# An attention and gated-FFN stage with a reordered opening, reordered rotations and maxima, and an earlier down piece

## The chip, the cores and the metric

The kernel runs on one core of one Trainium2 chip. The metric is the device time of one execution in microseconds (us); lower is better. Of several executions the median is taken.

## The reference, cut to what matters

A block of two layers over 4 x 1024 tokens of width 256. Only the second layer is touched by the change: a windowed attention with rotary embedding over 16 heads of 16, and a gated FFN whose hidden values are made 2-of-4 sparse by magnitude.

```python
x = layernorm(x + mamba_and_mlp(x))               # not touched
x = layernorm(x + mixture_of_experts(x))          # not touched except for its last layernorm
q, k, v = x @ w_q.T, x @ w_k.T, x @ w_v.T         # 16 heads of 16
q, k = rope(q), rope(k)                           # q*cos + rotated(q)*sin
attn = softmax(where(mask, q @ k.T * 0.25, -inf))
x = layernorm(x + (attn @ v) @ w_o.T)
h = silu(x @ w_gate) * (x @ w_up)                 # 1024 hidden values
h = keep_2_of_each_4_by_magnitude(h)
x = layernorm(x + h @ w_down)
```

## The kernel before, in words

The program has three phases; the third, `attention_ffn_phase`, is the one that changes. It writes out five instruction streams by hand, one for each engine, and orders them with semaphores. It works through four batches (`b` = 0 to 3) of 8 tiles of 128 tokens.

**Names.** For a tile `t` of batch `c`: `x_high` (ScalarE) and `x_low` (VectorE) split the input rows into two f16 parts; `x_transposed` (TensorE) transposes them and `xt_copied` (ScalarE) copies that out; `qkv` (TensorE, 12 matmuls at L1864) makes q, k and v; `qkv_copied` (ScalarE) evicts them; `rotate` (VectorE, four instructions, L1583 to L1590) applies the rotary embedding into the tile `ro`; `high_part` and `part_copies` (ScalarE) and `low_parts` (VectorE, L1596, L1597) write the split parts into `qks`. `first_rows` transposes them for the first head group. `for_maximum` (TensorE) makes one block of scores for the running row maximum and `maximum` (VectorE, L1607 and L1612) reduces it; a group of heads has 2 x `NX` = 40 of them, and the PSUM tile that they use has two halves, so that `for_maximum(m)` waits for `maximum(m - 2)`. `max_parts` closes each twenty. `weight_high` (ScalarE) and `weight_low` (VectorE, L1569) split the weights, which lie raw in the scratch tile `room`.

**The opening.** Before batch 0 there is nothing to overlap with. VectorE makes two layernorms (`stats`, `normal`), whose inverse deviations come from GpSimd (`inverse_deviation`). GpSimd then fills constant columns of `v` and `qks` (L1353 to L1356). Eight tiles pass through the chain above, then `first_rows`, the 40 maxima of the first head group, and `heads(0)`.

**One batch.** `heads(b)` is the attention. Then come the output projection and 16 chunks of hidden values (`w` = 0 to 15): TensorE `hidden(b, w)` (12 matmuls at L2059 into a ring of two PSUM tiles), ScalarE `silu`, VectorE `hidden` (the gated product, L1660), ScalarE `magnitude`. A chunk's matmuls wait until the gated product of two chunks before is done. Each four chunks are sparsified on VectorE by `compare` (L1670 to L1672), `count` (L1677 to L1685) and `keep_largest` (L1694), together `sparsify`, and then feed a down piece, `down(b, k)` with 16 calls (32 matmul records at L2072), k = 0 to 3, which waits for `keep_largest` of the same k. Pieces 0 and 1 make the first half of the tokens, which `residual(b, 0)` adds; 2 and 3 the second. In batches 0 to 2 the qkv and rotations of the next batch are interleaved with chunks 0 to 7, and the 40 maxima of its first head group with the later chunks and down pieces. This is what `ahead` stands for; the last batch has none of it. On TensorE the callbacks `among_hidden`, `at_end_of_first` and `at_end_of_second` place single `for_maximum` calls between matmuls.

```python
if w == (12 if ahead else DOWN_AT):
    down(b, 0, nothing)
    down(b, 1, at_end_of_first)
hidden(b, w, among_hidden)
...
down(b, 2, nothing)
if ahead:
    wait(pe, hm_ok, 16 * c)
    q_max_transposed(c, 0, 0)
down(b, 3, at_end_of_second)
```

Of the kernel before, what the change touches and what calls it, by code (L numbers as in the profile page):

```python
# [1157 lines left out]
def attention_ffn_phase(nc, io, keep):  # L1158
    with ExitStack() as ctx:  # L1159
# [173 lines left out]
        def _(pool):  # L1333
# [14 lines left out]
            pool.memset(power[:], -0.5)  # L1348
# [17 lines left out]
        def _(act):  # L1366
# [28 lines left out]
            def high_part(c, t):  # L1395
# [77 lines left out]
            act.sem_inc(ev_ok, LEAD)  # L1473
            weight_high(0, "w_qk")
# [4 lines left out]
            for t in range(ST):  # L1479
# [4 lines left out]
                if t in (1, 2):  # L1484
                    weight_high(t + 1, ("w_fg", "w_fu")[t - 1])
# [54 lines left out]
        def _(dve):  # L1540
# [36 lines left out]
            def rotate(c, t):  # L1577
# [180 lines left out]
            for t in range(ST):  # L1758
# [3 lines left out]
                low_parts(0, t)  # L1762
            weight_low(2, "w_fg")
            weight_low(3, "w_fu")
            maxima(0, 0, 0, 2 * NX)
            for b in range(NB):
# [21 lines left out]
                for w in range(NF + 1 if ahead else 16):  # L1788
                    if ahead and w + 1 < ST:
# [444 lines left out]
```

## Time and profile before

| what | value |
|---|---|
| median of 3 runs | 1815.56 us (1813.19 to 1816.39) |
| the profiled execution's own time | 1813.41 us |
| its span, first to last instruction | 1811.6 us |
| mean granted TensorE clock | 0.929 of 2.4 GHz |
| third phase | 687 to 1811.6 us |
| its opening, to the first scores of `heads(0)` | 687 to 787 us |

All times in the text are microseconds from the start of the span of the profiled execution. L1864 is line 1864 of the kernel. "Granted clock" is the share of TensorE's full clock that the chip granted: 1.00 is 2.4 GHz and 0.50 is 1.2 GHz. A row of the timeline merges instructions of one kind that ran back to back; a bracket behind it gives the engine's idle time before it and what released it.

### The profile page before, as it was taken

To read this page: it belongs to the slowest core of one execution; us is meant where nothing else is said; L and a number is where in the kernel's file an instruction comes from. 1 tells how busy PE (TensorE), PEld (TensorE's weight loads), DVE (VectorE), ACT (ScalarE), POOL (GpSimd) and SP (SyncE) were. 2 spreads that over 40 slices of the span, in tenths; PEclk is the share of its full clock that TensorE was granted. 3 is DMA by queue.
4 is the path that set the end of the run, shared out by engine and by line. 5 is a ranking of instruction groups with operands and counts; after the bars stand their busy time and mean duration, and the time that the engine had idled before them with its cause. 6 is when DMAs were issued, how large, how long until landed. Compare 5 with 4: busy or idle time off the path is not lost.

```text
span 1811.6 us, 27446 instructions
## 1 busy us (share of the span) xinstructions
PE 1542.5 (85%) x10490; PEld 961.8 (53%) x10491; DVE 1153.6 (64%) x2399; ACT 822.2 (45%) x1352; POOL 234.8 (13%) x237
## 2 busy tenths in 40 slices
PE   3999999977989973589888989888989888989796
PEld 2899988864568772233344534254534344433355
DVE  5566666637421145678568778668778678778475
ACT  5444444512212213347855157744157753177530
POOL 5334444412400001000000000100000100000000
PEclk8999999978999986669999989989999999989999
DMA  2000000105215502000000000000000000000000
GB/s 107 12 25 24 23 23 24 34 12 174 51 37 148 153 1 96 1 1 2 1 1 1 0 1 1 25 1 1 1 1 1 24 1 1 1 1 2 24 1 24
DMA packets 27153, 48.04 MB, mean 27 GB/s; under 512 B 7312, under 2 KB 16016, under 8 KB 26256
## 3 DMA queue, kind: packets, MB, share of 16 engines
q1 hardware_dynamic: 26464, 44.74, 7.7%
q0 software_dynamic: 576, 1.77, 0.4%
q8 instruction: 74, 1.21, 0.3%
q14 instruction: 39, 0.32, 0.1%
HBM read 37.59 MB, written 9.06 MB: 26 GB/s over the span
## 4 chain that ended last, share of the span: by engine, by line
issue 60%; POOL 2%; DVE 0%; POOLq 0%; DVEq 0%
POOL rs_sb L1340 1%; POOL ve_sb L1337 0%; POOL qks_sb L1355 0%; POOL v_sb L1354 0%; POOL qks_sb L1345 0%; DVE bn_sb L1545 0%; DVE x_sb_sb L1560 0%; POOLq L1159 0%; POOLq L65 0%; POOL qks_sb L1356 0%; DVE mv_sb L1551 0%; DVEq L1159 0%; POOL v_sb L1353 0%; DVE ident_h_sb L1742 0%; DVEq L65 0%
## 5 line engine op out<-in xcount | busy, mean ns | idle before, releaser
L1612 DVE TENSOR_REDUCE mx_sb<-s_ps 128x1 f32<-128x512 f32 (+1 forms) x512 | 312.8, 652 | 111.9 <-PE s_ps L1906 65.0
L1418 ACT ACTIVATE room_sb<-s_ps 128x1024 f32<-128x1024 f32 (+1 forms) x320 | 283.5, 949 | 23.7 <-PE s_ps L1930 22.5
L1903 PE MATMUL s_ps<-room_sb 48*128 48x512 f16 (+3 forms) x640 | 177.1, 343 | 39.9 <-DVE mx_sb L1607 20.0
L1903 PEld LDWEIGHTS s_ps<-room_sb 48*128 48x128 f16 x640 | 52.9, 96 | 210.3 <-DVE mx_sb L1612 126.4
L1930 PE MATMUL s_ps<-room_sb 51*128 51x128 f16 (+4 forms) x1152 | 145.3, 283 | 22.3 <-ACT room_sb L1418 14.9
L1950 PE MATMUL cm_ps<-room_sb,v_sb 128*32 128x512 f32 (+3 forms) x1536 | 162.3, 511 | 0.8 <-ACT room_sb L1424 0.8
L1337 POOL TENSOR_TENSOR ve_sb<-mv_sb,eps_sb 128x4 f32<-128x4 f32 x24 | 5.0, 210 | 1081.5 <-DVE mv_sb L1551 1081.5
L2072 PE MATMUL cm_ps<-w_fd_sb,room_sb 128*128 128x256 f32 x512 | 131.4, 406 | 14.7 <-DVE room_sb L1694 14.7
L394 DVE SCALAR_TENSOR_TENSOR x_sb_sb<-xp_sb,conv_w_sb,x_sb_sb 128x512 f32<-128x512 f32 x96 | 109.2, 1139 | 22.6 <-ACT x_sb_sb L319 20.5
L2072 PEld LDWEIGHTS cm_ps<-w_fd_sb,room_sb 128*128 128x128 f32 x512 | 97.3, 198 | 38.4 <-issue 14.0
L2059 PE MATMUL s_ps<-xbT_sb,w_fg_sb 128*128 128x512 f16 x384 | 100.3, 391 | 10.2 <-DVE ctok_sb L1660 8.7
L2059 PE MATMUL s_ps<-xbT_sb,w_fu_sb 128*128 128x512 f16 x384 | 103.3, 400 | 0.0
L965 PE MATMUL em_ps<-xT_sb,ws_gu_sb 128*128 128x512 f32 x192 | 90.4, 616 | 7.8 <-DMA rows<-zeros 7.8
L1930 PEld LDWEIGHTS s_ps<-room_sb 50*128 50x128 f16 (+1 forms) x1152 | 54.7, 97 | 79.0 <-ACT room_sb L1418 49.9
L1906 PE MATMUL s_ps<-room_sb 51*128 51x128 f16 x512 | 83.0, 233 | 10.5 <-ACT room_sb L1408 10.0
L400 DVE SCALAR_TENSOR_TENSOR m1T_sb<-mm_ps,m1T_sb 128x512 fp32r<-128x512 f32 x64 | 44.1, 688 | 66.1 <-ACT m1T_sb L311 65.8
L1464 ACT ACTIVATE sgl_sb<-s_ps 128x512 f32<-128x512 f32 x64 | 37.9, 593 | 85.5 <-PE s_ps L2059 85.3
L1607 DVE TENSOR_REDUCE mx_sb<-s_ps 128x2 f32<-128x512 f32 (+1 forms) x128 | 66.0, 554 | 13.3 <-PE s_ps L1906 13.0
L488 PE MATMUL ro_ps<-w_dn_sb,m1T_sb 128*128 128x256 f32 x256 | 71.6, 280 | 0.0
L489 PE MATMUL ro_ps<-w_dn_sb,m1T_sb 128*128 128x256 f32 x256 | 71.6, 280 | 0.0
L490 PE MATMUL ro_ps<-w_dn_sb,m1T_sb 128*128 128x256 f32 x256 | 71.5, 279 | 0.0
L311 ACT ACTIVATE m1T_sb<-mm_ps 128x512 fp32r<-128x512 f32 x64 | 37.9, 593 | 66.3 <-PE mm_ps L490 66.3
(255 smaller groups left out, 3194.6 us busy)
## 6 DMA issues: line engine op xcount, KB each, us to landing
we_gu_sb<-we_gu SPq DMA_DIRECT2D x32, 352.0 KB
we_dn_sb<-we_dn SPq DMA_DIRECT2D x32, 176.0 KB
x_in_sb<-x SPq DMA_DIRECT2D x9, 512.0 KB, 3.5
rows<-x_sb_sb SPq DMA_DIRECT2D x8, 512.0 KB, 3.0
x_sb_sb<-rows SPq DMA_DIRECT2D x2, 2048.0 KB, 12.0
out<-x_sb_sb SPq DMA_DIRECT2D x8, 512.0 KB, 2.6
xp_sb<-w_in SPq DMA_DIRECT2D x1, 1024.0 KB, 5.7
x_sb_sb<-w_up SPq DMA_DIRECT2D x1, 1024.0 KB, 7.3
```

The costliest lines, as they stand in the source:

```text
L394: dve.scalar_tensor_tensor(xc[:, c, :], xp[:, c, k:k + GTOK], conv_w[:, c, k:k + 1], xc[:, c, :], ALU.mult, ALU.add)\
L488: pe.matmul(out, of[0][at], by[0][cols], start=start, stop=False)
L489: pe.matmul(out, of[1][at], by[0][cols], start=False, stop=False)
L965: last = pe.matmul(mm[c % 4][:, :], ws_gu[:, k, col:col + P], xT[:, k, g * GTOK:(g + 1) * GTOK], start=(k == 0), stop=(k == KD - 1))
L1418: act.activation(weights[(g * NU + u) % SLOTS_P][:, 2 * pair:2 * pair + 2, 0:width(u) * P], W[s % 2][:, :, 0:width(u) * P], ACT.Exp, scale ...
L1612: dve.tensor_reduce(mx[:, pair, k % 2, slot:slot + 1], X[:, k % 2, 0:count * P], AX.X, ALU.max, negate=True).then_inc(mx_ok, 1)
L1903: last = pe.matmul(X[:, k % 2, at * P:(at + plain) * P], query[head:head + NORM, i * P:(i + 1) * P], key[head:head + NORM, j * P:(j + plai ...
L1906: last = pe.matmul(X[:, k % 2, (at + plain) * P:(at + count) * P], query[head:head + USED, i * P:(i + 1) * P], key[head:head + USED, i * P ...
L1930: last = pe.matmul(W[s % 2][:, head, (at + low - i) * P:(at + high - i) * P], key[first:first + rows, j * P:(j + 1) * P], query[first:firs ...
L1950: last = pe.matmul(O[32 * h:32 * h + 32, (i - half * GT) * P:(i - half * GT + count) * P], v[:, j, g * HG + h, :], weights[(g * NU + u) % ...
L2059: last = pe.matmul(bank[:, e, :], wt[:, j, k, ch * P:(ch + 1) * P], xh[:, g, k, i, :], start=(k == n == 0), stop=(k == KD - 1 and n == 2))
L2072: last = pe.matmul(CM[:, t // 2, (t % 2) * D:(t % 2 + 1) * D], hs[:, k % 3 * 4 + i, t * P:(t + 1) * P], w_fd[:, k % 2 * 4 + i, :], start=( ...
```

## The change

1. Opening, fills: the four fills of `v` and `qks` go from GpSimd's memsets to ScalarE activations, ahead of its first weight copy.
2. Opening, order on VectorE: the first half's layernorm, the second half's statistics, then `x_low` of tiles 0 and 1, the two weight parts, and only then the second half's `normal`.
3. Opening, tiles: rotated tiles alternate between `ro` and the tile `sgl`, so that `low_parts` of tile t - 1 stands behind `rotate` of tile t on VectorE.
4. Opening, FFN weights: the copies `weight_high` 2 and 3 go from among the tiles to behind the first four `qk_copied` on ScalarE; `weight_low` 2 and 3 go from ahead of the first twenty maxima to behind them on VectorE.
5. Batches 0 to 2, chunks 5 and 6: VectorE makes the gated product before the rotation. `keep_largest` of the first four chunks goes from behind product 6 to behind product 7.
6. Batches 0 to 2: TensorE makes down piece 0 ahead of chunk 10 (before: ahead of chunk 12, next to piece 1). No maxima stand among chunks 10 and 11. Maxima 0 to 7 stand in the second half of down piece 1, 8 to 23 among chunks 12 to 15, 24 to 39 in all of down piece 3 (before: 0 to 7 among chunks 10 and 11, 8 to 11 in the last quarter of piece 1, 12 to 27 among chunks 12 to 15, 28 to 39 in three quarters of piece 3). VectorE's order follows.

```diff
@@ gpsimd
-            pool.memset(v[:, :, :, HD:HD + 1], 1.0)
-            pool.memset(v[:, :, :, HD + 1:], 0.0).then_inc(setup, 1)
-            pool.memset(qks[:, :, :, USED:], 0.0)
-            pool.memset(qks[:, :, :, NORM:FILTER], UNIT).then_inc(setup, 1)
@@ scalar
+            def filled(out, value):
+                own = power[:, 0:1].unsqueeze(2).unsqueeze(3).to_broadcast([P, ST, out.shape[2], out.shape[3]])
+                return act.activation(out, own, ACT.Copy, scale=value / POWER)
+            act.wait_ge(setup, 1)
+            filled(v[:, :, :, HD:HD + 1], 1.0)
+            filled(v[:, :, :, HD + 1:], 0.0).then_inc(setup, 1)
+            filled(qks[:, :, :, USED:], 0.0)
+            filled(qks[:, :, :, NORM:FILTER], UNIT).then_inc(setup, 1)
             weight_high(0, "w_qk")
...
-                if t in (1, 2):
-                    weight_high(t + 1, ("w_fg", "w_fu")[t - 1])
...
                 for s in (1, 0):
                     qk_copied(0, 0, pair, s)
+            weight_high(2, "w_fg")
+            weight_high(3, "w_fu")
@@ vector
+        def turned_tile(c, t):
+            return sgl[:, 0, :].rearrange("p (h d) -> p h d", h=2 * HEADS) if c == 0 and t % 2 else ro[:, :, :]
...
-                wait(dve, ca_ok, k)
-                wait(dve, low_ok, k)
+                wait(dve, ca_ok, k if c > 0 else k - 1)
+                wait(dve, low_ok, k if c > 0 else k - 1)
...
-            for s in range(2):
-                layernorm("x", 0, s)
+            layernorm("x", 0, 0)
+            stats("x", 0, 1)
+            x_low(0, 0)
+            x_low(0, 1)
             weight_low(0, "w_qk")
             weight_low(1, "w_v")
-            x_low(0, 0)
-            x_low(0, 1)
+            normal("x", 0, 1)
...
                 rotate(0, t)
-                low_parts(0, t)
+                if t > 0:
+                    low_parts(0, t - 1)
+            low_parts(0, ST - 1)
+            maxima(0, 0, 0, NX)
             weight_low(2, "w_fg")
             weight_low(3, "w_fu")
-            maxima(0, 0, 0, 2 * NX)
+            maxima(0, 0, NX, 2 * NX)
...
-                    if ahead and w + 1 < ST:
+                    if ahead and w < TURN_LATE:
                         rotate(c, w + 1)
...
                     hidden(b, w)
+                    if ahead and TURN_LATE <= w < ST - 1:
+                        rotate(c, w + 1)
...
-                    if w >= 4 and w % 4 == 2:
+                    if w >= 4 and w % 4 == (3 if ahead else 2):
                         keep_largest(b, w // 4 - 1)
...
-                    for w in range(10, 12):
-                        m = 4 * (w - 10)
-                        maxima(c, 0, m, m + 2)
-                        hidden(b, w - 1)
-                        if w == 10:
-                            keep_largest(b, 1)
-                        maxima(c, 0, m + 2, m + 4)
+                    hidden(b, 9)
+                    keep_largest(b, 1)
+                    hidden(b, 10)
                     hidden(b, 11)
                     sparsify(b, 2)
-                    maxima(c, 0, 8, 12)
+                    maxima(c, 0, 0, 8)
                     residual(b, 0)
                     for w in range(12, 16):
-                        m = 4 * (w - 9)
+                        m = 4 * (w - 10)
...
-                    maxima(c, 0, 28, 2 * NX)
+                    maxima(c, 0, 24, 2 * NX)
@@ tensor
-                    if ahead and w in (10, 11):
-                        for_maximum(c, 0, 4 * (w - 10) + i)
                     if ahead and w >= 12:
-                        for_maximum(c, 0, 4 * (w - 9) + i)
+                        for_maximum(c, 0, 4 * (w - 10) + i)
...
-                    if ahead and t == GT - 1:
-                        for_maximum(c, 0, 8 + i)
+                    if ahead and t >= GT - 2:
+                        for_maximum(c, 0, 4 * (t - GT + 2) + i)
...
-                    if ahead and t > 0:
-                        for_maximum(c, 0, 28 + 4 * (t - 1) + i)
+                    if ahead:
+                        for_maximum(c, 0, 24 + 4 * t + i)
...
+                    if ahead and w == FIRST_DOWN:
+                        down(b, 0, nothing)
+                    if not ahead and w == DOWN_AT:
+                        down(b, 0, nothing)
                     if w == (12 if ahead else DOWN_AT):
-                        down(b, 0, nothing)
                         down(b, 1, at_end_of_first)
```

The constants are `TURN_LATE = 5`, `FIRST_DOWN = 10`, `POWER = -0.5`, and `GT` is 4. `high_part`, `part_copies` and `low_parts` read `turned_tile(c, t)` where they read `ro`.

## Rows read from the trace of the kernel before

**Rows 1.** The page: busy time, share of the span and instructions of each engine.

```profile
PE 1542.5 (85%) x10490; PEld 961.8 (53%) x10491; DVE 1153.6 (64%) x2399; ACT 822.2 (45%) x1352; POOL 234.8 (13%) x237
```

**Rows 2.** Stretches: length; busy PE, PEld, DVE, ACT, POOL; clock, DMA, GB/s.

```profile
704.50:755.30 50.80, 27.61 (x128) 13.94 (x128) 25.68 (x65) 26.13 (x56) 0.00 (x0) 0.70 0.00 0
...
755.30:787.00 31.70, 25.23 (x114) 9.44 (x115) 27.27 (x44) 4.90 (x5) 0.00 (x0) 0.50 0.00 1
...
970.30:994.50 24.20, 18.55 (x101) 7.46 (x100) 20.65 (x38) 10.10 (x17) 0.00 (x0) 0.86 0.00 1
...
1027.20:1053.00 25.80, 22.45 (x94) 14.08 (x92) 17.62 (x28) 2.11 (x3) 0.00 (x0) 0.93 0.00 1
```

**Rows 3.** Timeline of the opening, VectorE: start, length, line, tile, count.

```profile
696.38 6.20 DVE L1560 TENSOR_SCALAR x_sb_sb<-x_sb_sb,mv_sb,rs_sb 128x256 f32<-128x256 f32 x4 [1.49 <-POOL rs_sb L1340]
...
702.50 1.21 DVE L1569 SCALAR_TENSOR_TENSOR w_qk_sb<-room_sb,w_qk_sb 128x1024 f16<-128x1024 f32 x1
...
704.23 0.75 DVE L1575 TENSOR_TENSOR xs_sb<-x_sb_sb,xs_sb 128x256 f16<-128x256 f32 x2
```

**Rows 4.** Timeline of the opening, GpSimd: the longest of its fills.

```profile
698.07 2.87 POOL L1355 MEMSET qks_sb<- 128x3328 f16 x1
```

**Rows 5.** Line 1560 over the whole span: ns min/median/max, first and last start.

```profile
L1560 DVE TENSOR_SCALAR x_sb_sb<-x_sb_sb,mv_sb,rs_sb x96: 395/408/5173, 691.6 to 1808.2; 128x256 f32<-128x256 f32 x96
```

**Rows 6.** Timeline of the opening, ScalarE: two weight copies.

```profile
691.72 1.06 ACT L1369 ACTIVATE w_qk_sb<-room_sb 128x1024 f16<-128x1024 f32 x1 [43.89 <-DMA room_sb<-w_v]
...
712.11 1.92 ACT L1369 ACTIVATE w_fg_sb<-room_sb 128x2048 f16<-128x2048 f32 x1
```

**Rows 7.** Timeline of the opening's tiles, TensorE (in brackets: idle before, releaser).

```profile
706.53 2.77 PE L1864 MATMUL s_ps<-w_qk_sb,xt_sb 128*128 128x512 f16 x6
...
736.05 0.61 PE L1851 MATMUL s_ps<-ident_h_sb,xs_sb 128*128 128x128 f16 x4 [2.61 <-DVE xs_sb L1575]
...
736.45 2.77 PE L1864 MATMUL s_ps<-w_qk_sb,xt_sb 128*128 128x512 f16 x6
...
739.01 1.49 PE L1864 MATMUL s_ps<-w_v_sb,xt_sb 128*128 128x256 f16 x6
...
743.34 1.46 PE L1864 MATMUL s_ps<-w_qk_sb,xt_sb 128*128 128x512 f16 x6
```

**Rows 8.** Timeline of the opening's tiles, VectorE.

```profile
741.96 0.42 DVE L1596 TENSOR_TENSOR qks_sb<-ro_sb,qks_sb 128x256 f16<-128x256 f32 x1 [3.96 <-ACT qks_sb L1399]
...
742.63 0.42 DVE L1575 TENSOR_TENSOR xs_sb<-x_sb_sb,xs_sb 128x256 f16<-128x256 f32 x1
...
744.63 0.42 DVE L1590 TENSOR_TENSOR ro_sb<-ro_sb,sn_sb 128x256 f32<-128x256 f32 x1
```

**Rows 9.** Timeline after the last tile, VectorE: weight part, then maxima.

```profile
754.95 2.29 DVE L1569 SCALAR_TENSOR_TENSOR w_fg_sb<-room_sb,w_fg_sb 128x2048 f16<-128x2048 f32 x1
...
763.43 10.65 DVE L1612 TENSOR_REDUCE mx_sb<-s_ps 128x1 f32<-128x384 f32 x16
```

**Rows 10.** Timeline of batch 0's hidden chunks, TensorE, chunk 8.

```profile
973.36 2.72 PE L2059 MATMUL s_ps<-xbT_sb,w_fg_sb 128*128 128x512 f16 x6 [2.90 <-DVE ctok_sb L1660]
```

**Rows 11.** Timeline of batch 0, TensorE: down pieces and around them.

```profile
981.00 1.06 PE L1870 MATMUL s_ps<-ident_h_sb,qks_sb 128*128 128x128 f16 x16
...
994.53 12.79 PE L2072 MATMUL cm_ps<-w_fd_sb,room_sb 128*128 128x256 f32 x58
...
1010.43 0.82 PE L2059 MATMUL s_ps<-xbT_sb,w_fg_sb 128*128 128x512 f16 x3
...
1027.22 7.17 PE L2072 MATMUL cm_ps<-w_fd_sb,room_sb 128*128 128x256 f32 x32
...
1038.19 4.01 PE L2072 MATMUL cm_ps<-w_fd_sb,room_sb 128*128 128x256 f32 x10 [3.35 <-DVE room_sb L1694]
...
1042.45 0.70 PE L2072 MATMUL cm_ps<-w_fd_sb,room_sb 128*128 128x256 f32 x2
...
1043.41 0.70 PE L2072 MATMUL cm_ps<-w_fd_sb,room_sb 128*128 128x256 f32 x2
```

**Rows 12.** Timeline of batch 0, VectorE: product 9 and the third sparsification.

```profile
985.96 0.68 DVE L1660 SCALAR_TENSOR_TENSOR room_sb<-s_ps,sgl_sb 128x512 f32<-128x512 f32 x1
...
996.49 1.76 DVE L1670 TENSOR_TENSOR room_sb<-room_sb 128x1536 bf16<-128x1536 f32 x1 [0.69 <-ACT room_sb L1470]
...
1002.96 2.50 DVE L1694 SCALAR_TENSOR_TENSOR room_sb<-nb_sb,room_sb 128x512 f32<-128x512 bf16 x4
```

More of the change, by code:

```diff
@@ L1114 @@
 HALF_AT = 3
+TURN_LATE = 5
+FIRST_DOWN = 10
 DOWN_AT = 13
@@ L1127 @@
 W_SCALE = 64.0
+POWER = -0.5
 PRODUCTS = ((0, 0), (1, 0), (0, 1))
@@ L1346, in zero_columns @@
                 last.then_inc(zeroed, 1)
-            pool.memset(power[:], -0.5)
+            pool.memset(power[:], POWER)
             pool.memset(eps[:], 1e-5).then_inc(setup, 1)
@@ L1398, in high_part @@
                     wait(act, tm_mm, 2 * NHG * c)
-                act.activation(part(t, None, 0), ro[:, :, :], ACT.Copy).then_inc(a_ok, 1)
+                act.activation(part(t, None, 0), turned_tile(c, t), ACT.Copy).then_inc(a_ok, 1)
             def part_copies(c, t):
-                act.activation(part(t, 0, 2), by_head(ro[:, :, :])[:, :, 0, :, :], ACT.Copy)
-                act.activation(part(t, 1, 1), by_head(ro[:, :, :])[:, :, 1, :, :], ACT.Copy).then_inc(ca_ok, 1)
+                act.activation(part(t, 0, 2), by_head(turned_tile(c, t))[:, :, 0, :, :], ACT.Copy)
+                act.activation(part(t, 1, 1), by_head(turned_tile(c, t))[:, :, 1, :, :], ACT.Copy).then_inc(ca_ok, 1)
             def qk_copied(b, g, pair, s):
@@ L1580, in rotate @@
                 wait(dve, qkv_ok, k + 1)
-                wait(dve, ca_ok, k)
-                wait(dve, low_ok, k)
-                dve.tensor_tensor(ro[:, :, :], x, cos[:, t, :].unsqueeze(1).to_broadcast([P, 2 * HEADS, HD]),
+                wait(dve, ca_ok, k if c > 0 else k - 1)
+                wait(dve, low_ok, k if c > 0 else k - 1)
+                own = turned_tile(c, t)
+                dve.tensor_tensor(own, x, cos[:, t, :].unsqueeze(1).to_broadcast([P, 2 * HEADS, HD]),
                                   ALU.mult).then_inc(turned, 1)
@@ L1588, in rotate @@
                 wait(dve, turned, 2 * k + 2)
-                dve.tensor_tensor(ro[:, :, 0:HALF_D], ro[:, :, 0:HALF_D], sn[:, :, HALF_D:], ALU.add)
-                dve.tensor_tensor(ro[:, :, HALF_D:], ro[:, :, HALF_D:], sn[:, :, 0:HALF_D], ALU.add).then_inc(rv_ok, 1)
+                dve.tensor_tensor(own[:, :, 0:HALF_D], own[:, :, 0:HALF_D], sn[:, :, HALF_D:], ALU.add)
+                dve.tensor_tensor(own[:, :, HALF_D:], own[:, :, HALF_D:], sn[:, :, 0:HALF_D], ALU.add).then_inc(rv_ok, 1)
             def low_parts(c, t):
@@ L1594, in low_parts @@
                 wait(dve, rv_ok, c * ST + t + 1)
-                own = by_head(ro[:, :, :])
+                own = by_head(turned_tile(c, t))
                 dve.tensor_tensor(part(t, 0, 1), own[:, :, 0, :, :], part(t, 0, 0), ALU.subtract)
@@ L2100, in among_hidden @@
                         x_transposed(c, w + 2)
-                    if ahead and w in (10, 11):
+                    if ahead and w >= 12:
                         for_maximum(c, 0, 4 * (w - 10) + i)
-                    if ahead and w >= 12:
-                        for_maximum(c, 0, 4 * (w - 9) + i)
                 def at_end_of_first(t, i):
-                    if ahead and t == GT - 1:
-                        for_maximum(c, 0, 8 + i)
+                    if ahead and t >= GT - 2:
+                        for_maximum(c, 0, 4 * (t - GT + 2) + i)
                 def at_end_of_second(t, i):
-                    if ahead and t > 0:
-                        for_maximum(c, 0, 28 + 4 * (t - 1) + i)
+                    if ahead:
+                        for_maximum(c, 0, 24 + 4 * t + i)
                 heads(b)
```

## The prediction

> **What bounds the kernel.** I read the page first, for the engines' shares: TensorE is busy 85% of the span, VectorE 64%, ScalarE 45%, GpSimd 13% [rows 1]. That is an average, so I went on to stretches, and then to the timeline of each engine in the two places that the change touches.
>
> The opening is a chain and no engine is full. From 704.5 to 755.3 us TensorE is busy 27.6 of 50.8 us, VectorE 25.7, ScalarE 26.1 [rows 2]. The reader is to see what each waits for. A tile goes round one loop: its transposes wait for `x_low` (2.61 us idle), and VectorE can't give the next `x_low` because it stands in `low_parts`, 3.96 us idle for the `high_part` that ScalarE makes only after the next tile's qkv [rows 7, 8]. From 755.3 to 787 VectorE is busy 27.3 of 31.7 us with maxima and is the bound [rows 2, 9].
>
> In the batches TensorE is nearly full, and the losses are a few waits for VectorE: 2.90 us ahead of chunk 8 [rows 10], 24.2 us for 18.6 busy from there to down piece 0 [rows 2], and 3.35 us ahead of piece 3 [rows 11]. After such waits the granted clock is below 1.00 (0.86 and 0.93 in those stretches [rows 2]).
>
> **The opening's fills and order.** The second `normal` took 6.20 us for four instructions [rows 3], one of them 5.17 us where the median is 0.41 [rows 5]. That stretch is the one in which GpSimd fills, the longest fill being 2.87 us [rows 4]. VectorE was held by the fills, and this goes. (The Trainium skill, "SBUF — State Buffer", on the shared port pair, says that GpSimd and some VectorE instructions take it as an exclusive lock. The 5.17 us agree. The sum uses the row, so it would be the same without the page.) The fills now cost ScalarE: 1.06 us for 1024 elements and 1.92 for 2048 [rows 6] make some 0.2 us plus 0.84 per thousand; 128 + 1920 + 3328 + 512 elements in four instructions are 5.7 us, 5.4 with the overlap of neighbours. Bounds: nothing beyond its idle time until 691.72 [rows 6], or twice that if strided writes are slow, which would delay the first qkv by some 5 us. I take 5.4, since the rows are of the same kind. ScalarE then goes from 687.4 to 692.8, makes two weight copies to 694.4 and two `x_high` to 695.1. VectorE's statistics end at 694.9 (696.38 less 1.49 idle [rows 3]), `x_low` of two tiles at 695.6, and the two weight parts (702.50 to 704.23 [rows 3]) at 697.4. The first qkv starts at 697.5 instead of 706.53 [rows 7]: **9.0 us gained**.
>
> **The tiles.** With `low_parts` one tile late, VectorE's work per tile is `x_low` and the four rotation instructions, 742.63 to 744.97 with the last of 744.63 [rows 8], and `low_parts`, 741.96 to 742.63: 3.0 us, 3.15 with handovers. ScalarE's seven copies are 2.9. TensorE's tile is 4.45 us at the lower clock (0.4 for the transposes, then 736.45 to 740.5) and 2.2 at the higher, where the q and k part is 1.46 instead of 2.77 [rows 7]. So the period is 3.15 at 2.4 GHz and 4.45 at 1.2 GHz; before it was 6.2 to 7.1. Laid out from 697.5: the rotations of tiles 0 and 1 start at 702.25 and 704.7, six periods follow, and rotation 7, `low_parts` 6 and 7 take 3.5. At the higher clock the last `low_parts` ends at 727.1, at the lower at 734.9. The granted clock was 0.70 over this stretch [rows 2], so I take the middle, 3.8 a period: 731. That is 33.5 us instead of 48.5 (706.53 to 755.0): **15.0 us gained**, bounds 11 and 19. (The Trainium skill, "TensorE: Matmul & The Clock Gate", Part 1, says that the array is at half rate until activity releases it. Taken by itself it would have the denser loop at the higher clock, and the gain 19; no row before shows this loop dense.)
>
> **The FFN weights.** The two `weight_low` of 2.29 us [rows 9] stood where VectorE would have waited for the transposes and copies of q and k in any case. Now they stand between the twentieth and the twenty-first maximum. There maxima follow each other without a gap, 16 in 10.65 us [rows 9], and TensorE can be only two ahead. What is queued behind is the second twenty, then `heads(0)`. **4.4 us lost.** The ScalarE copies, 3.8 us, are hidden: their next work, `q_max_copied`, waits some 13 us for the first twenty maxima. Opening in all: -9.0 - 15.0 + 4.4 = **-19.6**, bounds -24 and -15.
>
> **Gated products ahead of rotations.** Product 5 ahead of rotation 6 puts that rotation, and through ScalarE's queue the next `silu`, some 0.7 us later; product 6 ahead of rotation 7 takes 2.0 us (one rotation, [rows 8]) from ahead of it. Net, product 6 comes 1.3 us earlier. Chunk 8 starts at 972.0 instead of 973.36 [rows 10]. Then `keep_largest` stands ahead of product 8, and `count` of the second four ends at 986.5, so product 9 is at 986.5 instead of 985.96 [rows 12]. The 1.4 us gained on TensorE are real there, and end in the next wait.
>
> **Down piece 0 ahead of chunk 10.** Batch 0 laid out: chunk 9 and its transposes end at 980.7 (before 981.9 [rows 11]). `keep_largest` of the first four is long done, so piece 0 fills 980.7 to 987.75 (7.05 us: 7.17 in [rows 11] with its modelled end). Chunks 10 and 11 take 2.6 each, to 992.95. Piece 1 starts there. Its first half and two slots with maxima are done at 998.1, and maximum 2 waits for VectorE's reduction of maximum 0. That stands behind product 11 (994.3) and all of the third sparsification: `compare` from 995.0 instead of 996.49, 8.97 us as before (996.49 to 1005.46 [rows 12]), to 1003.95. TensorE idles **6.2 us** in the middle of piece 1. Five slots of 0.95 us (1042.45 to 1043.41 [rows 11]) with what is left of this one bring piece 1's end to 1009.3. The row of chunk 12 before is 1010.43. The other waits of this size before, 2.90 and 3.35 us, were each followed by slow matmuls: 2.72 us for six after the first, against 1.46, and 4.01 us for ten records after the second, where a piece runs 32 in 7.17 [rows 10, 11]. I take 1.8 us for that, and chunk 12 at 1011.1. So the 5.6 us of waits that go from ahead of piece 0 come back inside piece 1. Bounds for chunk 12 against before: -1.1 (no slow matmuls) and +0.7 us; I take +0.3.
>
> **The moved maxima.** Chunks 12 to 15 get larger maxima: +0.2. Piece 3 gets four more: a slot with a maximum is 0.95 us, one without is 7.05 / 16 = 0.44, so +2.0. They were in chunks 10 and 11 beside waits; piece 3 has nothing to hide them. The wait ahead of piece 3 stays, since the sparsification follows product 15 as before. Each of batches 0, 1 and 2 (the same waits stand in all three) costs 0.3 + 0.2 + 2.0 = 2.5, **+7.5** in all; bounds +3 (by -1.1) and +9 (by +0.7), widened to 0 and +12 for waits that my layout may miss. Batch 3 has no edit.
>
> **Sum.** -19.6 + 7.5 = **-12.1 us** on an execution of 1813.41 (1.8 of it outside the span). The median of the runs is 2.15 above that one, so I forecast 1815.56 - 12.1 = 1803.5.
>
> **Rivals.**
> The forecast has chance 0.50: opening about -20, batches +2 to +3 each; 1800 to 1808.
>
> *The batches are neutral and the tiles run at 2.4 GHz* (0.27). For it: at 743.34 the clock did rise though TensorE waited in every period [rows 7], and the 9.7 us of idle and slow time between chunk 8 and piece 0 are more than the 6.2 that I put in. Against it: the third sparsification is fixed by product 11. It gives -24 + 1 = -23, 1792.
>
> *The tiles stay at 1.2 GHz and the fills are slow* (0.14). For it: clock 0.50 through 755 to 787 with TensorE 80% busy [rows 2]. It gives -9 - 11 + 4.4 + 3 = -12.6 for the opening; with +9 for the batches -3.6, 1812.
>
> *Slower than before* (0.08): the stall inside piece 1. If the clock stays at the lower level after the 6.2 us, through the 16 quarters of chunks 12 to 15, each quarter of 1.07 us grows by 0.7, 11 us a batch, 33 in all. It decides from 6.5 us a batch. Against it: after 3.35 us idle the clock was back within ten records [rows 11]. It gives -19.6 + 7.5 + 33 = +21, 1836.
>
> *No change* (0.01): it needs the tile loop to have another bound than `low_parts`; the 3.96 us wait speaks against that.
>
> **Chances.** A measurement here tells 0.2%, 3.6 us, from no change. Faster: 0.50 + 0.27 + most of 0.14 = 0.88. Same 0.04, slower 0.08. The range takes in the first three cases but their tails: 1790 to 1812.
>
> **What would show it.** First qkv near 697.5; no `normal` instruction over 0.5 us there; last `low_parts` 27 to 34 us after it; a gap of 4.4 us in the maxima; `heads(0)` 20 us earlier. In batch 0, relative to chunk 7: a wait of some 6 us inside piece 1, on a maximum; piece 3 some 15 us long with 16 maxima; each batch 2 to 3 us longer. The prediction is wrong if that wait is absent or the clock stays down behind it, or if the fills hold ScalarE beyond 695 us.

## The result, and the profile after

The changed kernel took 1852.7 us in the median (four runs, 1841.2 to 1854.5) against 1814.9 for the kernel before: ratio 1.0163, 95% interval 1.0126 to 1.0201. That is 30 us slower by the ratio and 38 by the two medians, where 12 us faster was forecast. Beside the experiments below the kernel before had medians of 1818.6 to 1821.5 us, so they are compared by their ratios to it. The page of the kernel after, its span and its first part:

```profile
span 1852.6 us, 27445 instructions
...
PE 1594.9 (86%) x10490; PEld 981.2 (53%) x10491; DVE 1151.2 (62%) x2399; ACT 827.1 (45%) x1356; POOL 229.6 (12%) x233
```

TensorE is busy 52 us more [rows 1] for the same 10490 instructions; VectorE has 2 us less. The mean granted clock is 0.898 instead of 0.929.

Where the time went is read from GpSimd, whose small `ve` instruction marks every layernorm. The timeline of GpSimd, kernel after: the start of the third phase, the first layernorm inside `heads(0)`, and the first ones inside `heads(1)` to `heads(3)`:

```profile
693.41 0.10 POOL L1355 MEMSET power_sb<- 128x4 f32 x1 [51.41 <-POOLq L615]
...
885.43 0.20 POOL L1344 TENSOR_TENSOR ve_sb<-mv_sb,eps_sb 128x4 f32<-128x4 f32 x1 [182.45 <-DVE mv_sb L1563]
...
1158.15 0.20 POOL L1344 TENSOR_TENSOR ve_sb<-mv_sb,eps_sb 128x4 f32<-128x4 f32 x1 [241.90 <-DVE mv_sb L1563]
...
1444.80 0.20 POOL L1344 TENSOR_TENSOR ve_sb<-mv_sb,eps_sb 128x4 f32<-128x4 f32 x1 [243.12 <-DVE mv_sb L1563]
...
1731.52 0.20 POOL L1344 TENSOR_TENSOR ve_sb<-mv_sb,eps_sb 128x4 f32<-128x4 f32 x1 [243.18 <-DVE mv_sb L1563]
```

The same marks before stand at 687.19, 902.92, 1157.96, 1426.13 and 1690.21. So the first two phases, which nothing touches, took 6.2 us more in this execution; the opening and `heads(0)` up to the mark took 192.0 us instead of 215.7, **23.7 us less**; and the three stretches between the marks took 17.7, 18.5 and 22.6 us more, **58.8 us in all**. 6.2 - 23.7 + 58.8 is 41.3, the difference of the two spans (41.0) to within 0.3 us.

**The opening after.** TensorE, kernel after, answering to [rows 7]:

```profile
703.64 2.72 PE L1879 MATMUL s_ps<-w_qk_sb,xt_sb 128*128 128x512 f16 x6
...
713.80 0.40 PE L1866 MATMUL s_ps<-ident_h_sb,xs_sb 128*128 128x128 f16 x4 [0.66 <-DVE xs_sb L1587]
...
717.23 0.40 PE L1866 MATMUL s_ps<-ident_h_sb,xs_sb 128*128 128x128 f16 x4 [1.09 <-DVE xs_sb L1587]
...
733.76 1.87 PE L1885 MATMUL s_ps<-ident_h_sb,qks_sb 128*128 128x128 f16 x16 [5.79 <-DVE qks_sb L1610]
```

VectorE, kernel after, answering to [rows 3, 9]:

```profile
703.41 1.37 DVE L1572 TENSOR_SCALAR x_sb_sb<-x_sb_sb,mv_sb,rs_sb 128x256 f32<-128x256 f32 x4
...
752.71 2.28 DVE L1581 SCALAR_TENSOR_TENSOR w_fg_sb<-room_sb,w_fg_sb 128x2048 f16<-128x2048 f32 x1
754.91 2.28 DVE L1581 SCALAR_TENSOR_TENSOR w_fu_sb<-room_sb,w_fu_sb 128x2048 f16<-128x2048 f32 x1
```

ScalarE's fills, kernel after:

```profile
693.58 2.03 ACT L1479 ACTIVATE v_sb<-power_sb 128x128 f32<-128x128 f32 x2 [40.04 <-POOL eps_sb L1356]
695.51 3.50 ACT L1479 ACTIVATE qks_sb<-power_sb 128x3328 f16<-128x3328 f32 x2
```

The first qkv starts 10.2 us behind the phase's start instead of 19.3. The second `normal` takes 1.37 us. The fills are 5.3 us of ScalarE (693.58 to 698.89). Tiles go by in 3.0 and 3.4 us, all but the first at the higher clock. `first_rows` starts 40.4 us behind the phase's start instead of 68.2. The two FFN weight parts stand in the maxima, 752.71 to 757.11.

**A batch after.** Stretches of the kernel after; columns as in [rows 2]. They are the opening's tiles, piece 1 to the end of its wait, the rest of piece 1, chunks 12 to 15, and piece 3:

```profile
703.60:733.80 30.20, 19.63 (x121) 10.78 (x122) 25.65 (x66) 21.55 (x53) 0.00 (x0) 0.90 0.08 32
974.99:986.55 11.56, 5.73 (x27) 4.05 (x26) 9.94 (x18) 1.23 (x2) 0.00 (x0) 0.87 0.00 0
986.55:995.09 8.54, 8.54 (x26) 3.68 (x27) 3.33 (x6) 0.00 (x0) 0.00 (x0) 0.50 0.00 0
995.09:1014.50 19.41, 19.41 (x77) 5.52 (x76) 13.60 (x23) 3.68 (x7) 0.00 (x0) 0.86 0.00 1
...
1025.61:1052.60 26.99, 26.99 (x61) 9.98 (x61) 10.15 (x16) 0.00 (x0) 0.00 (x0) 0.50 0.00 0
```

TensorE around them, kernel after, answering to [rows 10, 11]:

```profile
954.44 1.46 PE L2074 MATMUL s_ps<-xbT_sb,w_fg_sb 128*128 128x512 f16 x6 [1.48 <-DVE ctok_sb L1673]
...
974.99 4.05 PE L2087 MATMUL cm_ps<-w_fd_sb,room_sb 128*128 128x256 f32 x18
...
986.55 0.28 PE L1918 MATMUL s_ps<-room_sb 48*128 48x128 f16 x1 [5.83 <-DVE mx_sb L1620]
...
987.08 1.22 PE L2087 MATMUL cm_ps<-w_fd_sb,room_sb 128*128 128x256 f32 x2
...
1025.61 1.22 PE L2087 MATMUL cm_ps<-w_fd_sb,room_sb 128*128 128x256 f32 x2 [3.48 <-DVE room_sb L1707]
...
1027.19 1.22 PE L2087 MATMUL cm_ps<-w_fd_sb,room_sb 128*128 128x256 f32 x2
```

VectorE there, kernel after, answering to [rows 12]:

```profile
977.20 1.76 DVE L1683 TENSOR_TENSOR room_sb<-room_sb 128x1536 bf16<-128x1536 f32 x1 [0.69 <-ACT room_sb L1473]
...
983.66 2.49 DVE L1707 SCALAR_TENSOR_TENSOR room_sb<-nb_sb,room_sb 128x512 f32<-128x512 bf16 x4
986.08 0.75 DVE L1620 TENSOR_REDUCE mx_sb<-s_ps 128x2 f32<-128x256 f32 x2
```

The reader is to see two numbers. Behind the wait of 5.83 us inside piece 1 each call of the piece is 1.22 us where it was 0.70 ahead of it, and the matmuls stay slow up to the fourth quarter of chunk 12. And **piece 3 takes 26.99 us at a granted clock of 0.50 from its first call to its last**, against 14.91 us before (1038.19 to 1053.10). With chunk 7 as the common start (967.71 before, 950.21 after), batch 0 lost 2.2 us up to chunk 12, 2.6 in chunks 12 to 15 (19.41 instead of 16.79), 0.1 in piece 2 and its wait, and 12.1 in piece 3: 17.0 of 17.7. In all three batches together piece 3 lost 36 of the 58.8 us. (Piece 3 took 15.0 us in each batch before and 27.0 in each after, counted to the transposes behind it.)

The row of piece 3 shows TensorE busy 26.99 of 26.99 us. Busy time says nothing there of the pace. (The Trainium skill, "Trainium Kernel Development and Optimization", Performance Expectations, calls matmul busy time a bad metric for how close a kernel is to roofline. This piece agrees: fully busy both times, 14.9 and 27.0 us.)

### The profile page after: what moved, and what is told of

It reads as the page before. It is cut to its first block, busy times and chain, and to the rows that moved or that the text cites. A ratio compares the mean times of both kernels' runs of the same rounds, so it can differ in the third digit from the quotient of the medians.

```text
span 1852.6 us, 27445 instructions
## 1 busy us (share of the span) xinstructions
PE 1594.9 (86%) x10490; PEld 981.2 (53%) x10491; DVE 1151.2 (62%) x2399; ACT 827.1 (45%) x1356; POOL 229.6 (12%) x233
## 4 chain that ended last, share of the span: by engine, by line
issue 60%; POOL 2%; DVE 0%; POOLq 0%; DVEq 0%
POOL rs_sb L1347 1%; POOL ve_sb L1344 0%; DVE bn_sb L1557 0%; POOL qks_sb L1352 0%; DVE x_sb_sb L1572 0%; POOLq L1162 0%; POOLq L65 0%; DVE mv_sb L1563 0%; DVEq L1162 0%; DVE ident_h_sb L1755 0%; DVEq L65 0%; DVEq L1561 0%; DVEq L1754 0%; DVEq L1753 0%; DVEq L1752 0%
## 5 line engine op out<-in xcount | busy, mean ns | idle before, releaser
L1625 DVE TENSOR_REDUCE mx_sb<-s_ps 128x1 f32<-128x512 f32 (+1 forms) x512 | 313.7, 652 | 145.2 <-PE s_ps L1921 79.6
L1918 PE MATMUL s_ps<-room_sb 48*128 48x512 f16 (+3 forms) x640 | 189.5, 363 | 54.3 <-DVE mx_sb L1620 35.0
L2087 PE MATMUL cm_ps<-w_fd_sb,room_sb 128*128 128x256 f32 x512 | 166.1, 468 | 15.0 <-DVE room_sb L1707 15.0
L2087 PEld LDWEIGHTS cm_ps<-w_fd_sb,room_sb 128*128 128x128 f32 x512 | 104.9, 222 | 49.1 <-issue 25.4
L394 DVE SCALAR_TENSOR_TENSOR x_sb_sb<-xp_sb,conv_w_sb,x_sb_sb 128x512 f32<-128x512 f32 x96 | 109.2, 1140 | 22.6 <-ACT x_sb_sb L319 20.5
L1921 PE MATMUL s_ps<-room_sb 51*128 51x128 f16 x512 | 88.5, 245 | 6.3 <-ACT room_sb L1411 5.9
L1620 DVE TENSOR_REDUCE mx_sb<-s_ps 128x2 f32<-128x512 f32 (+1 forms) x128 | 66.2, 553 | 24.0 <-PE s_ps L1921 23.7
L1411 ACT ACTIVATE room_sb<-s_ps 128x1024 f16<-128x1024 f16 x24 | 23.2, 1023 | 104.1 <-PE s_ps L1885 104.1
## 6 DMA issues: line engine op xcount, KB each, us to landing
x_sb_sb<-rows SPq DMA_DIRECT2D x2, 2048.0 KB, 11.4
```

The lines of the kernel that those rows point to most:

```text
L394: dve.scalar_tensor_tensor(xc[:, c, :], xp[:, c, k:k + GTOK], conv_w[:, c, k:k + 1], xc[:, c, :], ALU.mult, ALU.add)\
L1625: dve.tensor_reduce(mx[:, pair, k % 2, slot:slot + 1], X[:, k % 2, 0:count * P], AX.X, ALU.max, negate=True).then_inc(mx_ok, 1)
L1918: last = pe.matmul(X[:, k % 2, at * P:(at + plain) * P], query[head:head + NORM, i * P:(i + 1) * P], key[head:head + NORM, j * P:(j + plai ...
L1921: last = pe.matmul(X[:, k % 2, (at + plain) * P:(at + count) * P], query[head:head + USED, i * P:(i + 1) * P], key[head:head + USED, i * P ...
L2087: last = pe.matmul(CM[:, t // 2, (t % 2) * D:(t % 2 + 1) * D], hs[:, k % 3 * 4 + i, t * P:(t + 1) * P], w_fd[:, k % 2 * 4 + i, :], start=( ...
```

## The experiments

**The two halves apart.** First the opening's edits alone: parts 1 to 4 as in the change, the batches as in the kernel before.

> The opening's edits alone (parts 1 to 4), batches as before. In the profile after, the first layernorm inside heads(0) stands 23.7 us earlier relative to the start of the third phase (192.0 instead of 215.7 us), while the batches lose some 60. Theory A (the opening's gain is real and independent of the batches): faster than before by 22 to 25 us. Rival B (part of that gain is given back once heads(0) starts): 5 to 15 us faster, or none.

Measured: 1794.5 us, ratio 0.9855 (0.9817 to 0.9893), 26 us faster. GpSimd's marks:

```profile
687.71 0.10 POOL L1355 MEMSET power_sb<- 128x4 f32 x1 [49.81 <-POOLq L615]
...
878.86 0.20 POOL L1344 TENSOR_TENSOR ve_sb<-mv_sb,eps_sb 128x4 f32<-128x4 f32 x1 [181.58 <-DVE mv_sb L1563]
```

191.2 us from the phase's start to the mark, 24.6 less than before. Theory A holds; the opening's gain is kept.

Then parts 5 and 6 alone behind the old opening.

> Parts 5 and 6 alone, opening as before. Theory A (losses come from the batches, 17.7, 18.5 and 22.6 us in the profile after): 55 to 65 us slower than before. Rival B (the two halves of the change interact, and the batches lose less behind the old opening): under 45 us slower.

Measured: 1870.2 us, ratio 1.0284 (1.0245 to 1.0324), 52 us slower: a little under the 55 that theory A allowed, well above B's 45. The first mark stands 216.4 us behind the phase's start (215.7 before), and the three stretches between the marks are 20.1, 15.2 and 19.3 us longer than before. With -26 the halves give +25, and together they measured +30 with intervals of some 7 us to either side: they add up.

This run also shows something that the changed kernel doesn't. Piece 3 of its batches 1 and 2 begins with one call at the higher clock, right behind the wait, and is slow from the second call on; 15 of the 16 calls take 1.22 us. TensorE, batch 1:

```profile
1330.60 0.70 PE L2072 MATMUL cm_ps<-w_fd_sb,room_sb 128*128 128x256 f32 x2 [3.48 <-DVE room_sb L1696]
...
1331.50 1.22 PE L2072 MATMUL cm_ps<-w_fd_sb,room_sb 128*128 128x256 f32 x2
```

**Is it the clock or the number of maxima?** The kernel before with one edit, on TensorE: the same 12 maxima, a quarter of the piece earlier.

```diff
 def at_end_of_second(t, i):
-    if ahead and t > 0:
-        for_maximum(c, 0, 28 + 4 * (t - 1) + i)
+    if ahead and t < GT - 1:
+        for_maximum(c, 0, 28 + 4 * t + i)
```

> The kernel before with one edit on TensorE: the 12 maxima in down piece 3 stand in its first three quarters instead of its last three. The number of instructions, of maxima and of waits is the same. Theory A (with a maximum behind each call from the first on, TensorE stays at 1.2 GHz after the wait ahead of piece 3, where four calls without maxima had let the clock rise): piece 3 takes some 23 us instead of 14.9, and the run is 20 to 30 us slower than before. Rival B (piece 3 is long because it has 16 maxima and their handovers, not 12): no change beyond 3 us.

Measured: 1838.2 us, ratio 1.0117 (1.0071 to 1.0163), 21 us slower. TensorE, batch 0 of this run, piece 3, and its stretch with columns as in [rows 2]:

```profile
1037.59 1.22 PE L2072 MATMUL cm_ps<-w_fd_sb,room_sb 128*128 128x256 f32 x2 [3.35 <-DVE room_sb L1694]
...
1039.28 1.22 PE L2072 MATMUL cm_ps<-w_fd_sb,room_sb 128*128 128x256 f32 x2
...
1057.84 3.54 PE L2072 MATMUL cm_ps<-w_fd_sb,room_sb 128*128 128x256 f32 x8
...
1037.60:1061.40 23.80, 23.80 (x52) 9.90 (x52) 8.89 (x15) 0.00 (x0) 0.00 (x0) 0.51 0.00 0
```

Twelve maxima and sixteen calls as before, and the piece takes 23.8 us (1037.59 to 1061.38) instead of 14.9, at 1.22 us a call and 1.69 a slot until the calls without maxima come. Rival B is out, and VectorE is not the bound: its reductions take 0.69 us and wait some 1.0 us for TensorE before each. Only the place of the four bare calls differs: first before, last here.

Next, 14 matmuls whose results nobody reads, in the changed kernel's wait ahead of piece 3.

```diff
+def spin(times):
+    for n in range(times):
+        pe.matmul(S[0][:, 0, :], w_fg[:, 0, 0, 0:P], xh[:, 0, 0, 0, :], start=True, stop=True)
 ...
     q_max_transposed(c, 0, 0)
+    spin(14)
 down(b, 3, at_end_of_second)
```

> The changed kernel with 14 extra matmuls of 512 columns on TensorE, whose results are not used, in the 3.5 us wait ahead of down piece 3 of batches 0 to 2. Theory A (the clock): the wait is filled, TensorE enters piece 3 at 2.4 GHz, piece 3 takes 15 to 16 us instead of 27, and the run is 30 to 36 us faster than the changed kernel, 1817 to 1823. Rival B (maxima and handovers): piece 3 stays at 25 us or more, and the run is within 3 us of the changed kernel or slower.

Measured: 1818.7 us, ratio 0.9994 (0.9958 to 1.0030), 31 us under the changed kernel by the ratios. TensorE, batch 0 of this run:

```profile
1016.68 3.19 PE L2115 MATMUL s_ps<-xbT_sb,w_fg_sb 128*128 128x512 f16 x14
1020.32 0.70 PE L2087 MATMUL cm_ps<-w_fd_sb,room_sb 128*128 128x256 f32 x2 [0.46 <-DVE room_sb L1707]
...
1034.36 0.70 PE L2087 MATMUL cm_ps<-w_fd_sb,room_sb 128*128 128x256 f32 x2
```

The idle time ahead of the piece shrinks to 0.46 us, every call of the piece is 0.70 again, and the piece with its 16 maxima takes 15.2 us, in all three batches. Some 30 us of the 59 were the clock in piece 3 alone.

The same filling in the kernel before with the maxima in front:

> The run with the kernel before's 12 maxima in the first three quarters of down piece 3, plus 14 unused matmuls of 512 columns in the wait ahead of that piece. Theory A (the clock alone made that kernel slow): piece 3 takes 14 us or less and the run is back at the level of the kernel before or up to 6 us faster. Rival B (maxima ahead in the piece cost by their place): it stays 10 us or more slower than before.

Measured: 1816.4 us, ratio 0.9972 (0.9934 to 1.0010): back at the level of before. TensorE, batch 0 of this run, and the stretch of the piece:

```profile
1038.03 0.70 PE L2072 MATMUL cm_ps<-w_fd_sb,room_sb 128*128 128x256 f32 x2 [0.33 <-DVE room_sb L1694]
...
1049.43 1.99 PE L2072 MATMUL cm_ps<-w_fd_sb,room_sb 128*128 128x256 f32 x8
...
1038.00:1051.30 13.30, 13.27 (x48) 6.19 (x48) 8.91 (x15) 0.00 (x0) 0.00 (x0) 1.00 0.00 0
```

11.4 us for the twelve slots and 13.4 for the piece, at a granted clock of 1.00 where it was 0.51. The same order of calls is 10.4 us shorter by the filling alone.

**The wait inside piece 1.** The changed kernel with both waits filled.

```diff
 def at_end_of_first(t, i):
+    if ahead and t == GT - 2 and i == 2:
+        wait(pe, hm_ok, 16 * b + 11)
+        spin(26)
```

(The `wait` makes sure that the product has been read from the PSUM tile that the unused matmuls overwrite. The 14 of the run before stay.)

> The changed kernel with unused matmuls in both waits: 14 ahead of down piece 3, as in the run before this, and 26 in the wait for maximum 0 inside down piece 1. The wait inside piece 1 lasted 5.8 us and was followed by 14 us at 1.2 GHz, to the middle of chunk 12. Theory A (the rest of the loss is clock too): piece 1 goes on at 2.4 GHz, 5 to 7 us less for each batch, and the run is 15 to 20 us faster than with the first filling alone, 1799 to 1804. Rival B (only piece 3 was a clock matter; piece 1 is bound by the reductions on VectorE): within 4 us of 1819.

Measured: 1799.0 us, ratio 0.9884 (0.9860 to 0.9908), 20 us below the first filling. TensorE, batch 0 of this run:

```profile
975.12 5.78 PE L2115 MATMUL s_ps<-xbT_sb,w_fg_sb 128*128 128x512 f16 x26
...
981.45 0.70 PE L2087 MATMUL cm_ps<-w_fd_sb,room_sb 128*128 128x256 f32 x2
...
986.01 0.82 PE L2074 MATMUL s_ps<-xbT_sb,w_fg_sb 128*128 128x512 f16 x3
```

Calls of 0.70 us right behind the wait, and chunk 12 at 986.01, where it is 995.09 in the changed kernel with a third phase that began 5.2 us later: 3.9 us earlier within the phase. Chunks 12 to 15 take 17.0 us instead of 19.4, so this is 6.3 us a batch, as A said. What TensorE has to wait for comes no sooner: from the first unused matmul to `for_maximum(2)` it is 6.0 us, since that time is VectorE's.

With both waits filled the kernel is at 0.9884, and the opening alone without any filling was at 0.9855 (0.9817 to 0.9893). So even at the higher clock parts 5 and 6 show no gain.

**Piece 3's first quarter without maxima, no fillings.** The four maxima go to piece 1. The cut shows TensorE; VectorE's order follows.

```diff
 def at_end_of_first(t, i):
-    if ahead and t >= GT - 2:
-        for_maximum(c, 0, 4 * (t - GT + 2) + i)
+    if ahead and t > 0:
+        for_maximum(c, 0, 4 * (t - 1) + i)
 def at_end_of_second(t, i):
-    if ahead:
-        for_maximum(c, 0, 24 + 4 * t + i)
+    if ahead and t > 0:
+        for_maximum(c, 0, 28 + 4 * (t - 1) + i)
```

> The changed kernel, down piece 0 still ahead of chunk 10, but with the four maxima taken out of the first quarter of piece 3: piece 1 has maxima 0 to 11 in its last three quarters, chunks 12 to 15 have 12 to 27, piece 3 has 28 to 39 in its last three quarters as in the kernel before. No extra matmuls. Theory A: piece 3 takes 15 us again instead of 27 and the run is 25 to 36 us faster than the changed kernel, 1817 to 1828, what is left being the wait and the slow clock in piece 1. Rival B (the early piece 0 is what costs, through the wait in piece 1): little changes, 1840 or more.

Measured: 1836.6 us, ratio 1.0086 (1.0066 to 1.0107), 14 us under the changed kernel. That is between the two expectations. TensorE, batch 0 of this run: the first slow call in piece 1, chunk 12, and piece 3:

```profile
987.57 1.22 PE L2087 MATMUL cm_ps<-w_fd_sb,room_sb 128*128 128x256 f32 x2
...
1002.33 1.46 PE L2074 MATMUL s_ps<-xbT_sb,w_fg_sb 128*128 128x512 f16 x3
...
1032.53 4.63 PE L2087 MATMUL cm_ps<-w_fd_sb,room_sb 128*128 128x256 f32 x10 [3.35 <-DVE room_sb L1707]
...
1047.54 0.70 PE L2087 MATMUL cm_ps<-w_fd_sb,room_sb 128*128 128x256 f32 x2
```

Piece 3 is 16 us instead of 27; A said 15. But piece 1 now waits 7.56 us instead of 5.83, has nine slow calls in place of five, and lasts to 1002.33, which is 6.8 us later behind the phase's start. Of the 11 us that piece 3 won, piece 1 lost 7: the maxima moved from one slow stretch into another.

**Part 5 alone.** Gated products ahead of rotations, in the kernel before.

> Part 5 alone in the kernel before: gated products 5 and 6 ahead of rotations, and keep_largest of the first four chunks behind product 7. By the layout in the prediction chunk 8 starts 1.4 us earlier and the gain ends in the next wait. Theory A: within 3 us of before. Rival B (a shorter wait ahead of chunk 8, 1.5 us where it was 2.9, keeps the clock at 2.4 GHz and this carries on): 3 to 8 us faster.

Measured: 1824.5 us, ratio 1.0020 (1.0000 to 1.0040). TensorE, batch 0 of this run: chunk 8, and piece 3's start:

```profile
979.91 1.46 PE L2062 MATMUL s_ps<-xbT_sb,w_fg_sb 128*128 128x512 f16 x6 [1.48 <-DVE ctok_sb L1661]
...
1045.61 4.11 PE L2075 MATMUL cm_ps<-w_fd_sb,room_sb 128*128 128x256 f32 x10 [3.35 <-DVE room_sb L1695]
```

The wait ahead of chunk 8 is 1.48 us instead of 2.90 and its six matmuls take 1.46 us instead of 2.72 [rows 10]. Nothing of this is left in the total, which is the same or slightly longer: piece 3 comes 65.7 us behind chunk 8 here, 64.8 before, so the next waits took back 0.9 us of it (those inside chunks 10 and 11 are 3.7 us together, 2.7 before), and the rest doesn't show.

**The opening's parts.** Part 1 alone:

> Part 1 alone in the kernel before: the four fills as ScalarE activations, VectorE's order as before. Theory A (GpSimd's fills held the second normal, 6.20 us for 1.38 of work, and ScalarE's fills cost less than that): the second normal takes 1.4 us, the weight parts and the first qkv come 4 to 5 us earlier, the run is 3 to 5 us faster than before, at the edge of what can be told. In the profile the first layernorm inside heads(0) stands 211 us behind the start of the third phase instead of 215.7. Rival B (normal is slow for another reason, or the longer ScalarE queue delays the splits): 0 to 2 us.

Measured: 1816.2 us, ratio 0.9976 (0.9950 to 1.0003). VectorE, the second `normal` of this run:

```profile
703.07 1.38 DVE L1565 TENSOR_SCALAR x_sb_sb<-x_sb_sb,mv_sb,rs_sb 128x256 f32<-128x256 f32 x4 [1.49 <-POOL rs_sb L1340]
```

The mark stands 210.1 us behind the phase's start (693.88 to 904.02), 5.6 less than before, a little over A's 5; the total is at the edge of what can be told. In the kernel before the one long `normal` instruction ran from 696.38 to 701.55, and GpSimd's second to fourth fill, back to back, from 696.38 to 701.40. So VectorE was held across three fills, not for the longest of 2.87 us alone [rows 4].

Part 3 alone:

> Part 3 alone in the kernel before: a second tile for the rotated rows in the opening, low_parts one tile late. The copies of the FFN weights stay among the tiles and ahead of the maxima. Theory A (the wait of VectorE in low_parts bounded the loop): the tile period falls from 6 to 7 us to 3.2 to 3.5 at the higher clock, first qkv to last low_parts from 48.5 to about 31 to 34 us; 14 to 18 us faster. Rival B (the weight copies among the tiles, 3.8 us of ScalarE, or the clock, become the bound): 10 us or less.

Measured: 1797.0 us, ratio 0.9884 (0.9823 to 0.9945), 21 us faster, where A said 14 to 18; the mark is 16.9 us nearer, and the rest is within the interval. TensorE: the longest period of a tile, 4.5 us, where the copies of the FFN weights stand among the tiles, and `first_rows`:

```profile
718.07 0.40 PE L1858 MATMUL s_ps<-ident_h_sb,xs_sb 128*128 128x128 f16 x4 [1.68 <-DVE xs_sb L1579]
...
722.55 0.40 PE L1858 MATMUL s_ps<-ident_h_sb,xs_sb 128*128 128x128 f16 x4 [2.13 <-DVE xs_sb L1579]
...
739.08 1.87 PE L1877 MATMUL s_ps<-ident_h_sb,qks_sb 128*128 128x128 f16 x16 [5.80 <-DVE qks_sb L1602]
```

First qkv (706.61) to `first_rows` is 32.5 us, inside A.

**Two versions for speed.** The opening alone with the waits ahead of chunk 8 and piece 3 filled:

> The opening's edits alone, batches as before, and unused matmuls in two waits of each batch: 12 ahead of chunk 8 (wait of 2.9 us), 14 ahead of down piece 3 (3.35 us). Theory A (slow matmuls behind a wait cost 1.3 us at chunk 8 and 2.2 us at piece 3): 8 to 11 us faster than the opening alone, about 1784 to 1787. Rival B (the slow stretches hide under other waits, as the gain of an earlier chunk 8 would): 3 us or less.

Measured: 1791.7 us, ratio 0.9833 (0.9787 to 0.9880). That is 4 us less than the opening alone, between A and B and within the spread of the runs. In the profile piece 3 takes 13.3 us in every batch, where it is 14.7, 15.0 and 16.3 in the opening alone, so that gain doesn't hide under later waits. But stretches of unchanged code around it ran at another clock: from the end of piece 3 of batch 1 to the next mark 109.6 us at a granted clock of 0.89, in the opening alone 106.1 at 0.94.

The last takes out part 4 as well, and keeps only the filling ahead of piece 3. Cut to part 4, against the changed kernel:

```diff
+                if t in (1, 2):
+                    weight_high(t + 1, ("w_fg", "w_fu")[t - 1])
...
-            maxima(0, 0, 0, NX)
             weight_low(2, "w_fg")
             weight_low(3, "w_fu")
-            maxima(0, 0, NX, 2 * NX)
+            maxima(0, 0, 0, 2 * NX)
```

> A version for speed: the opening's parts 1 to 3, with the FFN weight copies left among the tiles and weight_low left ahead of the maxima as in the kernel before (part 4 out), batches as before, and 14 unused matmuls in the wait ahead of down piece 3. Theory A (part 4 cost 4.4 us in the maxima and gives some 2.5 us back in the tiles; a warm start of piece 3 is worth some 2 us a batch): the first layernorm inside heads(0) stands 189 to 190 us behind the start of the third phase, against 191.2 for the opening alone, and the run is at 1786 to 1792. Rival B (the copies among the tiles cost as much as they save, and the slow start of piece 3 is hidden): no difference from the opening alone, 1794.

Measured: 1782.4 us (1779.3 to 1786.1), ratio 0.9802 (0.9779 to 0.9826), 36 us faster than before, and the fastest of all. GpSimd's marks:

```profile
687.26 0.10 POOL L1355 MEMSET power_sb<- 128x4 f32 x1 [48.41 <-POOLq L615]
...
876.41 0.20 POOL L1344 TENSOR_TENSOR ve_sb<-mv_sb,eps_sb 128x4 f32<-128x4 f32 x1 [179.58 <-DVE mv_sb L1563]
```

189.2 us between them, 2.0 less than for the opening alone, as expected. The total is below A's 1786 to 1792; the 2 us of the opening don't account for it. Between the marks this profile is 11.3 us shorter than that of the opening alone: 6.0 of it in the three pieces 3, the rest in stretches with the same code, of which the three ahead of the pieces ran at a granted clock of 1.00, 0.97 and 0.97 against 0.97, 0.94 and 0.96. Why that clock differs was not taken apart.

## Why the prediction was wrong

**The opening: right, step by step.** First qkv 9.0 us earlier was forecast, 9.1 measured. Fills 5.4 and 5.3. Tiles and all up to `first_rows`: forecast 24.0 in the middle and 28.0 at the higher clock, measured 27.8, so the loop ran at the higher clock, the upper bound. (The Trainium skill, "TensorE: Matmul & The Clock Gate", Part 1, has activity release the half rate; the loop agrees, with granted clock 0.90 where it was 0.70.) The two `weight_low` among the maxima: 4.4 forecast, 4.4 measured. In sum -23.7 instead of -19.6, within the bounds.

**Part 5: right that it comes to nothing.** Alone it measured 1.0020 (1.0000 to 1.0040).

**Down piece 0: the wait was right, what follows it too small.** A wait of 6.2 us on maximum 0 was forecast inside piece 1, 5.83 measured, released by the first maxima, which stand right behind the third sparsification. The 1.8 us for slow matmuls behind it, taken from rows where calls without maxima followed a wait, was the wrong price: the clock stayed down for 14 us (986.55 to about 1000.4). Chunk 12 was 2.2 us late where +0.3 was forecast, and chunks 12 to 15 took another 2.6 where +0.2 was.

**The moved maxima: this is the step that failed.** "Piece 3 gets four more: a slot with a maximum is 0.95 us" priced them from a row at 2.4 GHz. At that clock the price is right: 16 slots took 15.2 us with the wait filled. But before, the four calls without maxima at the head of piece 3 were what followed the wait of 3.35 us, and the clock rose in them (4.01 us for ten records, then 0.95 a slot [rows 11]). The change put maxima there, and the clock never rose: 16 slots at 1.69 or 1.58 us, 27.0 us instead of the 17 forecast, in each of three batches. The kernel before with its maxima moved to the front shows it with their number unchanged, and the fillings undo it in both kernels. What the moved work took away was the stretch in which TensorE had regained its clock. The prediction had named the sign itself: it called itself wrong if the clock stays down behind the wait inside piece 1, and it did, for 14 us, and behind the wait ahead of piece 3 to the end of the piece.

**The rivals.** The case "slower" (0.08) had the clock staying down behind a wait as its mechanism, and gave +21; measured +30 to +38. Its place was wrong: it named chunks 12 to 15, where the clock was back after some 5 of 19 us, and not piece 3, which has the short f16 maxima between its f32 calls. Its argument against itself, that after the wait ahead of piece 3 the clock was back within ten records, was the very thing that the change removed.

**What stays open.** Why a stretch with a maximum behind each call keeps the clock at 1.2 GHz though the profile has TensorE busy in all of it, while the twelve matmuls of a chunk or bare calls raise it. The runs show that it is so (piece 3 with the maxima in front, piece 3 of the changed kernel, the opening's maxima at 0.50 [rows 2]), not by what measure. (The Trainium skill, "TensorE: Matmul & The Clock Gate", Part 1, has activity release the half rate; rows of full busy time did not release it here, so the measurement decides.) With the fillings the same slots keep the higher clock, 0.70 a call through all of piece 3. But to begin the piece at the higher clock is not enough: in batches 1 and 2 of the run with parts 5 and 6 alone the first call took 0.70 and the next fifteen 1.22.

## What to carry to other kernels

Behind every wait of some microseconds on TensorE look at which work comes first, and at what clock the rows ran from which it is priced; a price from a stretch at 2.4 GHz holds only if the stretch is entered at 2.4 GHz. In down piece 3 calls with no small matmuls between them had to come first behind the wait, and only then the calls with small ones behind each. Where no such work is at hand, unused matmuls in the wait bought back 10 us a batch here, and moving the small matmuls elsewhere moved much of the loss.

## What the runs showed of the hardware

- One order of calls, two speeds: 12 slots of a down call and a maximum took 20.2 us entered after an idle 3.35 us and 11.4 us entered behind 14 spare matmuls, with the same instructions. VectorE waited for TensorE before each reduction in both, some 1.0 us and 0.26 us.
- A VectorE instruction of 0.41 us took 5.17 beside GpSimd's fills [rows 5]; with the fills on ScalarE none of the 96 was over 0.42. It was held across three fills in a row.
- The first two phases, the same in every kernel, ended between 686.9 and 694.6 us in the fourteen profiles of this study, so a single profile's span says nothing below 8 us; the marks inside the third phase say more.
- But unchanged code between the marks varies too, with the granted clock: from the first layernorm of `heads(1)` to piece 3 of batch 1 it took 149.2 us at 0.94 in the kernel before and in the opening alone, and 145.2 at 0.97 with part 1 alone.
